# The end of a kernel's first pass: smaller opening scatters, another order of its last loads, tables and stores, and part of a rounding correction moved from GpSimd to VectorE

## The reference

```python
# x: 16 sequences of 512 tokens of 256 features
x = x + layernorm(attn(layernorm(x)))      # q-shift, k/v/r projections, scan, gate, Wo
x = x + layernorm(moe(layernorm(x)))

def moe(x):                                # 8192 tokens
    scores = softmax(x @ gate_w.T + gate_b)            # 8 experts
    top_w, top_i = top_k(scores, 2)
    y = sum over the two chosen experts e of
        top_w[e] * ((silu(x @ w1[e].T + b1[e]) * (x @ w3[e].T + b3[e])) @ w2[e].T + b2[e])
    z = silu(x @ ws1.T + bs1) * (x @ ws3.T + bs3) @ ws2.T + bs2     # shared expert, 512 inner
    return y + z
```

## Time and profile before

| | us |
|---|---|
| median of 3 runs | 1110.96 (1108.74 to 1112.02) |
| the profiled execution, its own time | 1108.02 |
| its span, first to last instruction | 1106.2 |
| busy: PE / DVE / POOL / ACT | 982.5 / 879.5 / 779.7 / 561.6 |
| mean granted TensorE clock | 0.937 of full |

### The profile page before, as it was taken

One profiled execution on the slowest core, in us unless ns is written; L12 is line 12 of the kernel. 1 busy time (PEld: TensorE's weight loads), 2 busy tenths in 40 slices (PEclk: granted clock), 3 DMA queues, 4 the chain that ended last, 5 costly groups with the idle time before them and its releaser, 6 DMA issues. The chain is left out here.

```text
span 1106.2 us, 23285 instructions
## 1 busy us (share of the span) xinstructions
PE 982.5 (89%) x6344; PEld 876.6 (79%) x6344; DVE 879.5 (80%) x2225; ACT 561.6 (51%) x1020; POOL 779.7 (70%) x790
## 2 busy tenths in 40 slices
PE   3658999999999999999999958999999999998462
PEld 3547788888888888888888847999999999998341
DVE  6788999999999999999988735767776776776586
ACT  4355566556655665566555613344443444443365
POOL 2353987787779777877797661758766676767488
PEclk9679999999999999999999987999999999999555
DMA  6222443444344434443441493987778878886797
GB/s 197 67 79 93 139 144 97 143 148 135 105 140 148 138 101 142 148 132 105 144 129 58 156 290 75 212 228 124 114 132 192 214 115 218 199 203 111 235 399 296
DMA packets 108661, 172.72 MB, mean 156 GB/s; under 512 B 13869, under 2 KB 76744, under 8 KB 108360
## 3 DMA queue, kind: packets, MB, share of 16 engines
q1 hardware_dynamic: 76120, 119.68, 33.9%
q0 software_dynamic: 27744, 36.72, 19.0%
q10 hardware_dynamic: 4752, 15.80, 3.7%
HBM read 173.53 MB, written 76.86 MB: 226 GB/s over the span
## 5 line engine op out<-in xcount | busy, mean ns | idle before, releaser
L1944 POOL DMA_INDIRECT sum_y<-e_y,e_row_at x142 | 224.8, 1583 | 43.3 <-issue 39.7
L1778 PE MATMUL e_h_ps<-e_z_hi,w_room 128*128 128x256 f32 x1136 | 218.2, 284 | 9.2 <-DMA w_room<-w_split 7.5
L1778 PEld LDWEIGHTS e_h_ps<-e_z_hi,w_room 128*128 128x128 f32 x1136 | 182.1, 191 | 13.2 <-issue 10.6
L1822 ACT ACTIVATE e_act_h<-e_h_ps,w_room 128x256 f32<-128x256 f32 x142 | 67.4, 474 | 191.4 <-PE e_h_ps L1778 175.4
L1778 PE MATMUL e_h_ps<-e_z_lo,w_room 128*128 128x256 f32 x568 | 160.3, 282 | 0.0
L1543 POOL DMA_INDIRECT slots_x<-f_xf,f_at x120 | 136.6, 1139 | 31.9 <-issue 31.9
L1794 PE MATMUL e_y_ps<-w_room,e_h_hi 128*128 128x256 f32 x568 | 117.9, 291 | 1.3 <-DVE e_h_lo L1868 1.1
L1861 DVE SCALAR_TENSOR_TENSOR e_h<-e_h_ps,w_room,e_act_h 128x256 f32<-128x256 f32 x142 | 67.8, 482 | 63.9 <-ACT e_act_h L1822 61.8
L1116 DVE RECIPROCAL f_den<-f_den 128x256 f32<-128x256 f32 (+1 forms) x49 | 109.2, 2233 | 0.5
L1778 PEld LDWEIGHTS e_h_ps<-e_z_lo,w_room 128*128 128x128 f32 x568 | 108.5, 191 | 0.0
L642 PE MATMUL f_h_ps<-f_f_hi,f_w_hi 128*128 128x512 f32 x224 | 92.2, 412 | 5.5 <-DVE f_h_room L1149 3.1
(11 more groups left out here) (296 smaller groups left out, 2971.2 us busy)
## 6 DMA issues: line engine op xcount, KB each, us to landing
w_room<-w_split SPq DMA_DIRECT2D x73, 512.0 KB
w_room<-w_split SPq DMA_DIRECT2D x71, 514.0 KB
w_room<-w_split ACTq DMA_DIRECT2D x69, 512.0 KB
rows_room<-slots_x SPq DMA_DIRECT2D x71, 260.0 KB, 2.9
f_x_in<-x SPq DMA_DIRECT2D x16, 512.0 KB, 5.2
f_x_res<-x SPq DMA_DIRECT2D x16, 512.0 KB, 4.6
x_dram<-f_x_room SPq DMA_DIRECT2D x16, 512.0 KB, 2.9
sum_y<-f_y SPq DMA_DIRECT2D x32, 256.0 KB, 2.2
```

The costliest lines, as they stand in the source:

```text
L1778: last = pe.matmul(h_ps[q][:, which, :], w13(p, q, part)[:, which, c, :], z[p % 2][:, c, :], start=(n == 0), stop=(n == 5))
L1822: act.activation(act_h[q][:, :], h_ps[q][:, 0, :], ACT.Silu, bias=bias(p, 0, q)).then_inc(silu_ready, 1)
L1944: pool.indirect_dma_start(out=dst[:, :], out_offset=bass.IndirectOffsetOnAxis(ap=row_at[p][:, j:j + 1], axis=0), in_=y[p][:, j, :], in_off ...
```

## The change

1. **Opening scatters.** Eight scatters of 32 rows in place of 128. The rings p = 2, 3 now have spare rows of their own, so POOL no longer waits for the scatters of rings 0, 1 to land before it issues theirs.
2. **Stores of y.** The two halves of `y` of SECOND go through `x_res[1]`, a buffer that is free by then, and not through `y[0]`, `y[1]`. So ACT's read of LAST's `y` no longer waits for a store of SECOND to land. A new semaphore counts the two stores, and SP waits for it at its end; `expert_tiles` waits for one store less per buffer.
3. **SP's last queue.** Rows of tile 0 first, then weights of tile 0, and the rest in another order.
4. **DVE's end.** `tile_tables()` stands behind LAST's last product and low parts, not before them.
5. **Two of four low parts of h.** In every pass (and for THIRD in `finish`) q = 0 and 1 are subtracted by DVE, before `product(..., 2)`, and not by POOL. They count on a semaphore of their own.

```diff
@@ buffers
-        PAIR = SLOT_TILE // P
-        spare_row = sb("spare_row", [P, 2, PAIR])
-        spare_at = sb("spare_at", [P, 2, PAIR], mybir.dt.uint32)
+        PAIR, FEW = SLOT_TILE // P, 32
+        spare_row = den[0][:, 0:4 * PAIR].rearrange("p (a j) -> p a j", j=PAIR)
+        spare_at = sb("spare_at", [P, 4, PAIR], mybir.dt.uint32)
+        def late_y(s, half):
+            return x_res[1][:, half * 2:half * 2 + 2, :] if s == SECOND else y[half][:, :, :]
@@ SP
-            first_weights(0)
             sp.wait_ge(cleared, 16 * (E + 1))
...
             first_rows(0)
+            first_weights(0)
             first_rows(1)
-            store_y(SECOND, 1)
+            late_store_y(SECOND, 1)
+            first_rows(2)
+            late_store_y(LAST, 0)
             first_weights(1)
-            first_rows(2)
+            late_store_y(LAST, 1)
             first_rows(3)
-            store_y(LAST, 0)
-            store_y(LAST, 1)
+            sp.wait_ge(late_y_stored, 32)
@@ PE, outer and late_outer(THIRD)
-                    pe.wait_ge(hlo_ready, (s + 1) * Q)
+                    pe.wait_ge(first_hlo_ready, (s + 1) * 2)
+                    pe.wait_ge(hlo_ready, (s + 1) * 2)
@@ ACT, late_read_y
-                act.wait_ge(y_stored[half], 16 * s)
-                act.activation(y[half][:, :, :], late_y_ps[half], ACT.Copy).then_inc(y_read, 1)
+                if s == SECOND:
+                    act.wait_ge(x1_ready, SEQS)
+                else:
+                    act.wait_ge(y_stored[half], 16 * SECOND)
+                act.activation(late_y(s, half), late_y_ps[half], ACT.Copy).then_inc(y_read, 1)
@@ DVE
+            def first_h_low(s, q):
+                dve.wait_ge(hhi_ready, s * Q + q + 1)
+                dve.tensor_tensor(h_lo[:, q, :], h[q][:, :], h_hi[:, q, :].bitcast(F32), ALU.subtract)\
+                    .then_inc(first_hlo_ready, 1)
@@ DVE, body (and the same before product(THIRD, 2) in finish)
                 low_w(i)
+                first_h_low(i - 2, 0)
+                first_h_low(i - 2, 1)
                 product(i - 2, 2)
@@ DVE, end of finish
                 late_product(LAST, 2)
-                tile_tables()
                 late_product(LAST, 3)
                 late_low_h(LAST, 2)
                 late_low_h(LAST, 3)
+                tile_tables()
@@ POOL, begin_scatters
-                if p >= 2:
-                    pool.wait_ge(early["y_stored"][p - 2], 16 * PAIR)
                 for j in range(PAIR):
                     pool.indirect_dma_start(out=shared_y[:, :],
-                                            out_offset=bass.IndirectOffsetOnAxis(ap=spare_at[:, p % 2, j:j + 1], axis=0),
-                                            in_=nobody[:, 0, 0:C], in_offset=None, compute_op=ALU.add)\
+                                            out_offset=bass.IndirectOffsetOnAxis(ap=spare_at[0:FEW, p, j:j + 1], axis=0),
+                                            in_=nobody[0:FEW, 0, 0:C], in_offset=None, compute_op=ALU.add)\
@@ POOL, body (and the same in finish)
-                h_low(i - 2, 0)
-                h_low(i - 2, 1)
```

More of the change, by code:

```diff
@@ L338, in first_pass @@
         hlo_ready = sem("hlo_ready")
+        first_hlo_ready = sem("first_hlo_ready")
         late_hlo_ready = sem("late_hlo_ready")
@@ L342, in first_pass @@
         y_stored = early["shared_stored"]
+        late_y_stored = sem("late_y_stored")
         spare_ready = sem("spare_ready")
@@ L499, in _, with late_store_y @@
             clear_tails()
-            store_y(SECOND, 0)
+            def late_store_y(s, half):
+                sp.wait_ge(y_read, 2 * s + half + 1)
+                at = (s * 2 + half) * (T // 2)
+                sp.dma_start(by_tiles(shared_y[bass.ds(at, T // 2), :]), late_y(s, half))\
+                    .then_inc(late_y_stored if s == SECOND else y_stored[half], 16)
+            late_store_y(SECOND, 0)
             def first_rows(n):
@@ L1147, in product @@
                 dve.wait_ge(silu_ready, s * Q + q + 1)
-                wait(dve, hlo_ready, (s - 1) * Q + q + 1)
+                if q < 2:
+                    wait(dve, first_hlo_ready, (s - 1) * 2 + q + 1)
+                else:
+                    wait(dve, hlo_ready, (s - 1) * 2 + q - 1)
                 dve.scalar_tensor_tensor(out=h[q][:, :], in0=h3_ps[:, :], scalar=bias[:, 1, q:q + 1],
                                          in1=act_h[q % 2][:, :], op0=ALU.add, op1=ALU.mult).then_inc(h_ready, 1)
+            def first_h_low(s, q):
+                if not inside(s, SEQS):
+                    return
+                dve.wait_ge(hhi_ready, s * Q + q + 1)
+                dve.tensor_tensor(h_lo[:, q, :], h[q][:, :], h_hi[:, q, :].bitcast(F32), ALU.subtract)\
+                    .then_inc(first_hlo_ready, 1)
             def by_rows(v, n):
@@ L1245, in spare_rows @@
             def spare_rows():
-                for p in range(2):
-                    last = dve.tensor_scalar(spare_row[:, p, :], own_s[:, :], float(SEQS * T + p * SLOT_TILE), None, ALU.add)
+                for p in range(4):
+                    at = SEQS * T + p % 2 * SLOT_TILE + p // 2 * FEW * PAIR
+                    last = dve.tensor_scalar(spare_row[:, p, :], own_s[:, :], float(at), None, ALU.add)
                 last.then_inc(spare_ready, 1)
@@ L1362, in late_product @@
                 if s == SECOND:
-                    dve.wait_ge(hlo_ready, (s - 1) * Q + q + 1)
+                    dve.wait_ge(*((first_hlo_ready, (s - 1) * 2 + q + 1) if q < 2 else (hlo_ready, (s - 1) * 2 + q - 1)))
                 else:
@@ L1396, in finish @@
                 invert(LAST, 1, slice(0, T // 2))
+                first_h_low(THIRD, 0)
+                first_h_low(THIRD, 1)
                 product(THIRD, 2)
@@ L1588, in finish @@
                 inverse_std(LN_X1, SECOND, 0)
-                h_low(THIRD, 0)
-                h_low(THIRD, 1)
                 make_nobody()
@@ L1951, in _ @@
             for half in range(2):
-                pool.wait_ge(early["shared_stored"][half], 16 * early["sequences"])
+                pool.wait_ge(early["shared_stored"][half], 16 * (early["sequences"] - 1))
             def body(i, par):
```

## The result

The changed kernel takes **1102.88 us** (median of 20 runs, 1099.32 to 1109.70) against 1109.42 for the kernel before in the same comparison (20 runs, 1105.60 to 1117.58): ratio **0.9943, interval 0.9928 to 0.9957**, 6.3 us faster. The forecast was 7.4 us and 1103.5. A second comparison gave 1099.02 against 1106.95, ratio 0.9920 (0.9888 to 0.9953).

The account below looks back on a forecast made before the run. About 14 us of PE idleness at the first barrier, held by POOL's scatters, then SP's queue. The pass begins at 660.9 instead of 668.3, 7.4 us gained including 1.2 lost in finish: median 1103.5, range 1099.5 to 1108.5.

Parts of the forecast that it names:

- The step on the scatters' issue cost: POOL before the first barrier: a 32-row scatter takes 0.7 us to issue, bracket 0.39 to 1.55.
- SP's queue is the last: First barrier: SP drains at 660.6, after POOL's drain by 659.6 and PE at 652.7; the pass begins at 660.9.
- The first rival: First barrier: 32-row scatters cost what 128-row ones did, or the barrier waits for memory; gain 2.5 to 4.8; chance 0.2.
- SP's sum: SP's last queue: first issue at 650.6, 9.9 us of issues ending at 660.5, store landed at 659.9, drain at 660.6.
- Everything that follows is 1.2 later: After finish: two subtractions on DVE delay PE's chain, so scatters, tables and all that follows come 1.2 us later.
- A gain is excluded by PE's 20.00 of 20: Loop: fewer subtractions on POOL gain nothing, as POOL doesn't hold PE, which is busy 20.00 of 20 us.
- The 1.2 us in finish: finish: THIRD's two subtractions on DVE cost 1.2 us; PE's wait of 1.63 becomes 2.8.
- The low parts in the loop: Loop, DVE: two subtractions, at most 1.36 us, fit into the 1.32 us wait for ACT per pass; cost nil.
- The slower rival: Loop: POOL's layernorm chain holds DVE's subtractions, 10.9 us lost over 13 passes, giving 1114.5; chance 0.05.
- The tables: DVE's end: tables end 2.65 us later, costing SP 2.65; PE gains 2.7, worth nothing given its idleness.
- The late store: SP's end: SECOND's store lands 8.3 us after issue, not 5.5; gain 5.3, giving 1105.7; chance 0.12.
- The clock: Start of the expert pass: PE's clock probably still low, nothing booked, 1 us either way.

Follow-up runs that it names:

- changed_again: The changed kernel itself, unaltered, run once more for a second profile; 1099.02 us against 1106.95 for the kernel before, ratio 0.9920.
- lows_on_pool: The changed kernel with all low parts of h up to THIRD back on POOL; 1101.26 us against 1107.52 for the kernel before, ratio 0.9947.
- scatters_alone: The kernel before with only the scatters of 32 rows and each ring's own spare rows; 1099.55 us against 1107.52, ratio 0.9936.
- third_on_pool: The changed kernel with THIRD's two low parts in finish back on POOL, the loop's kept on DVE; 1096.07 us against 1107.52 before, ratio 0.9902.
- tables_back: The changed kernel with tile_tables ahead of LAST's last product again; 1096.82 us against 1107.52 for the kernel before, ratio 0.9903.
- one_each: The changed kernel with one opening scatter per ring instead of two, expert-pass counts from 16; 1099.09 us against 1106.96 before, ratio 0.9928.
- old_queue: The changed kernel with SP's issues in the order of before, their other edits kept; 1096.97 us against 1106.95 before, ratio 0.9909.
- four_early: The changed kernel with the scatters of rings 0 and 1 ahead of LAST's sends; 1096.33 us against 1106.95 before, ratio 0.9921.

## Why the prediction came out right, and where it did not

**The place and the size are right, the size by luck.** The gain is at the first barrier and was put at 7.4 us; changed_again opens it 6.8 us earlier, and the median moved by 6.3. The range held it. But two terms of the sum were wrong by more than 2.5 us each, and nearly cancelled.

**The step on the scatters' issue cost is wrong.** The prediction took 0.7 us, "nearer to the lower end", from a bracket of 0.39 to 1.55; it is 1.31. Eight of them span 11.4 us from first to last start and not 7.0. So "SP's queue is the last" is wrong too, for that profile: POOL still is, at 661.2 against 660.0. The first rival, "a scatter of 32 rows costs what one of 128 did", was nearly the truth, and its own turning point (0.9 to 1.1) was passed. The gain came out as forecast nevertheless, because the first scatter began earlier: forecast 644.9, measured 642.3. The errors of +4.4 on the span, -2.6 on the start and -0.2 on the time from the last issue to the drain make 1.6: the prediction's 659.6 for POOL became 661.2. SP's sum is right in the same way, 660.6 against 660.0: its first issue is 2.7 us earlier than forecast (647.9 for 650.6), its issues take 0.5 longer, and it then stands 1.7 us for a store that was to have landed.

**"Everything that follows is 1.2 later" is wrong.** PE is through at 650.1 (forecast 652.7), the last table row ends at 647.2 (649.8), the first scatter starts at 642.3 (644.9) and SP at 647.9 (650.6): all four stand 2.6 to 2.7 us before their forecast. They were to be 1.2 us later than before by change 5, and are 1.4 us earlier.

**"A gain is excluded by PE's 20.00 of 20" is wrong.** PE's weight loads did wait for POOL in the loop, 12 times for 3.5 us in all, which the list of waits shows in a row that the prediction didn't read. The windows' 20.00 counts a matmul as busy whose weights come late. Taking two subtractions off POOL gains 1.0 to 1.6 us in the loop (lows_on_pool, scatters_alone and before against the rest). Of the 1.4 us by which the scatters start earlier than before, that and the loss in finish leave about half (0.7, lows_on_pool against changed_again). The rest is what executions differ by: scatters_alone, without the move, starts them at 642.9.

**The 1.2 us in finish** are 1.0 against third_on_pool, and 0.5 against before, at LAST's `project`. At the first scatter none of the 1.0 is left in third_on_pool. The wait at the project of LAST grew from 1.63 to 2.17, not to 2.8. The prediction allowed 0 to 0.5 back from a less busy POOL, and took none.

**The low parts in the loop** fit into DVE's wait as worked out. The slower rival didn't happen: the contention is there, but it is POOL's small operations that are held (`f_rstd` 1.34 for 1.02) and not DVE's. The page "SBUF — State Buffer" of the Trainium skill, "Who interferes with whom", leaves both ways open, and which engine comes second decides; here that is POOL (`f_minus_mean` begins at 370.40, DVE's first subtraction at 370.31). ACT waits for the end of that chain, 13 times for 2.6 us in all, and PE doesn't.

**The tables** were priced rightly: counted from the first scatter, SP's first issue is 2.7 us later than before and 2.4 later than in tables_back, and PE is through 2.7 earlier. Neither reaches the barrier while POOL is last; where SP is last, as in one_each, the later issue stands in the way. Change 3 buys nothing either (old_queue), and change 2 has no run of its own. scatters_alone, with none of changes 2 to 5, opens the barrier at 661.8 and the changed kernel at 661.5; counted from the loop, scatters_alone is 1.1 us ahead, though it has no clock dip between the loop and the scatters and changed_again has one.

**The late store.** SP is released 8.4 us after the store's issue, about as late as before, and not 5.5. So that rival was true of the store and of no weight, since SP isn't last. The 5.5 was right for the old order of the queue (5.4 in scatters_alone, 5.7 in old_queue); it is change 3 that makes the store late again.

**The clock** was booked at nothing, with 1 us either way, and gave about 1.6 us in changed_again: 5.5 us of the pass at half clock, where it was 8.7. It is no firm gain: in the traces of the other changed kernels and in the first profile it is 5.6 to 8.5 us, so 0.1 to 1.6 us are given back.

## What to carry to other kernels

When several queues end at a barrier, work out the end of each and see which is last by how much: an edit to any other buys nothing. Here one of the five edits, the scatters, gave nearly the whole gain; the new order and the tables did not reach the barrier, and the low parts gave under 1 us. A cost that is only bracketed needs its whole bracket carried to the question "who is last", not the middle value. To shorten a row of small indirect DMAs, issue fewer of them; fewer rows in each hardly help. Read the waits of the weight loads as well as those of the matmuls before an engine is called fully busy. And before two traces are compared at their end, subtract how far one is ahead of the other where they still run the same code; here that took away nearly all of third_on_pool's 1.3 us, and 1.1 to 1.5 us of what four_early and one_each seemed to gain.

## What the runs showed of the hardware

POOL's indirect DMA with addition costs 1.31 to 1.33 us to issue for 8 or 32 rows, 1.41 for 64, 1.55 for 128. POOL's drain ends 0.9 to 1.1 us after the last such DMA has landed (ten traces). That is 6.7 to 8.3 us after its issue while SP's loads are in the queues, and 4.7 us after it in one_each, where the last scatter is issued at 645.6, ahead of SP's first load at 646.4. SP's drain takes 7 ns (13 in the first profile after), and before it began 0.3 us after SP had issued its last store (655.71 + 4.11); it doesn't wait for its own transfers. TensorE was granted half clock for 3.4 us once or twice between 100 us and the barrier's idleness in every trace (in tables_back for 6.8 us on end, from 644.2). Each time the clock falls within, or up to 6.4 us behind, an idleness of PE of 1.6 to 3.1 us: right behind the wait for `f_g_lo` at about 598 in six traces, behind that for ACT at 609 in third_on_pool. Not every such idleness is followed by a fall: of the eight traces in which that wait for `f_g_lo` is 2.2 us, the first profile after and tables_back have none there. Profiles of one kernel differed by 6.6 us, more than most edits are worth.
